# Layer 0's first chunk in split form, and the GpSimd queue written anew around it

## What is computed

```python
B, F, D = (512, 32, 32)
z = jnp.einsum('bhd,bmd->bhmd', x0, prev)   # x0: the gathered rows
z = z.reshape(b, h * m, d)
cur = jnp.einsum('bpd,pn->bnd', z, W[0])    # 128 maps
cur = jax.nn.relu(cur)
...
h = jnp.concatenate([z, dense_ctx], axis=1) # z: both layers summed over d
h = jnp.maximum(h @ W_top1 + b_top1, 0.0)
h = jnp.maximum(h @ W_top2 + b_top2, 0.0)
y = h @ W_top3
```

## Time and profile before

| | |
|---|---|
| median of 3 runs | 843.92 us |
| the profiled execution | 844.84 us |
| its span, first to last instruction | 843.0 us |
| mean granted TensorE clock | 1.00 (2.4 GHz) |
| TensorE busy (matmuls) | 835.0 us, 99% |
| TensorE weight loads busy | 672.6 us, 80% |
| VectorE busy | 770.2 us, 91% |
| ScalarE busy | 784.3 us, 93% |
| GpSimd busy | 723.5 us, 86% |
| DMA traffic | 60.19 MB, mean 71 GB/s |

### The profile page before, as it was taken

How to read it: one execution, slowest core, us unless ns; L and a number is a source line. 1 busy time by engine, 2 the same in 40 slices (tenths; PEclk the granted TensorE clock), 3 DMA queues, 4 the chain that set the end, 5 groups by cost and what they waited for, 6 DMA issues and landing times.

```text
span 843.0 us, 18638 instructions
## 1 busy us (share of the span) xinstructions
PE 835.0 (99%) x3595; PEld 672.6 (80%) x3595; DVE 770.2 (91%) x2029; ACT 784.3 (93%) x2779; POOL 723.5 (86%) x550
## 2 busy tenths in 40 slices
PE   9999999999999999999999999999999999999998
PEld 7688888888888888888888888888888888888777
DVE  7689999999999999999999999999999999999895
ACT  4799999999999999999999999999999999998985
POOL 5898888998888989888999888899888899987860
PEclk9999999999999999999999999999999999999999
DMA  5541233321233332133232123332123333212000
GB/s 150 185 118 38 74 79 85 83 84 42 53 83 80 82 84 57 36 84 78 82 84 71 31 75 78 83 84 82 38 58 82 80 83 84 51 44 77 0 14 1
DMA packets 62104, 60.19 MB, mean 71 GB/s; under 512 B 26203, under 2 KB 37083, under 8 KB 62078
## 3 DMA queue, kind: packets, MB, share of 16 engines
q1 hardware_dynamic: 57982, 57.80, 23.2%
q0 software_dynamic: 4096, 2.11, 4.0%
HBM read 55.51 MB, written 4.31 MB: 71 GB/s over the span
## 4 chain that ended last, share of the span: by engine, by line
PE 93%; POOL 2%; DMA 2%; issue 1%; DVE 1%; SPq 0%; ACT 0%; POOLq 0%; DVEq 0%
PE ps_y L898 26%; PE ps_y L906 26%; PE ps_y L899 26%; PE ps_c L871 3%; PE ps_c L881 3%; PE ps_c L879 2%; PE ps_c L880 2%; POOL gat L453 1%; PE ps_c L877 1%; DMA h_scratch<-h_sums 1%; POOL z L432 1%; DVE prod L728 0%; DMA w_raw<-w 0%; DMA gat<-table,rows 0%; DMA h<-h_scratch 0%
## 5 line engine op out<-in xcount | busy, mean ns | idle before, releaser
L565 ACT ACTIVATE prod<-ps_y,es 128x128 f32<-128x128 f32 x2560 | 723.9, 506 | 34.3 <-PE ps_y L906 27.1
L728 DVE SCALAR_TENSOR_TENSOR prod<-ps_y,es,prod 128x128 f32<-128x128 f32 x1536 | 424.6, 345 | 56.9 <-PE ps_y L906 53.3
L898 PE MATMUL ps_y<-w_hi,c_both 128*128 128x512 f32 x1024 | 415.1, 405 | 1.7 <-POOL w_lo L460 1.3
L906 PE MATMUL ps_y<-w_hi,c_both 128*128 128x512 f32 x1024 | 399.5, 390 | 0.0
L899 PE MATMUL ps_y<-w_lo,c_both 128*128 128x512 f32 x1024 | 399.2, 390 | 0.0
L442 POOL TENSOR_TENSOR prod<-prod 128x768 f32<-128x768 f32 x128 | 238.1, 1860 | 67.2 <-DVE prod L728 64.6
L740 DVE TENSOR_REDUCE csum<-prod 128x64 f32<-128x896 f32 x256 | 276.5, 1080 | 0.1
L898 PEld LDWEIGHTS ps_y<-w_hi,c_both 128*128 128x128 f32 x1024 | 192.4, 188 | 50.9 <-issue 10.3
L899 PEld LDWEIGHTS ps_y<-w_lo,c_both 128*128 128x128 f32 x1024 | 192.4, 188 | 49.4 <-issue 8.2
L906 PEld LDWEIGHTS ps_y<-w_hi,c_both 128*128 128x128 f32 x1024 | 192.2, 188 | 41.6
L432 POOL TENSOR_TENSOR z<-first,second 128x512 f32<-128x512 f32 x155 | 199.0, 1303 | 0.0
(11 more groups left out here) (119 smaller groups left out, 292.7 us busy)
## 6 DMA issues: line engine op xcount, KB each, us to landing
second<-et_scratch SPq DMA_DIRECT2D x155, 256.0 KB, 3.7
first<-et_scratch SPq DMA_DIRECT2D x31, 256.0 KB, 3.4
et_scratch<-gat SPq DMA_DIRECT2D x62, 64.0 KB
w_raw<-w SPq DMA_DIRECT2D x4, 512.0 KB
h_scratch<-h_sums SPq DMA_DIRECT2D x120, 2.0 KB
gat<-table,rows_now POOLq DMA_INDIRECT x116
wt_sb<-wt SPq DMA_DIRECT2D x2, 512.0 KB
rows_now<-rows SPq DMA_DIRECT2D x30, 2.0 KB, 1.8
```

Of the source, the lines that this page charges most:

```text
L565: last = nc.scalar.activation(prod[:, buffer_of(g, u), place // 2, :, place % 2], ps_y[:, bank_of(g, u, k), j * N:(j + 1) * N], ACT.Copy, ...
L728: last = nc.vector.scalar_tensor_tensor(out=summed, in0=ps_y[:, bank_of(g, u, k), j * N:(j + 1) * N], scalar=es[:, g.r, u, h:h + 1], in1=s ...
L898: nc.tensor.matmul(out, hi, w_hi, start=True, stop=False)
L906: nc.tensor.matmul(out, lo, w_hi, start=False, stop=True).then_inc(y_ready, 1)
```

## The change

Chunk 0 of layer 0 takes the split form as well (WHOLE = 0, so SPLIT = 5), which adds a `z_hi` on ScalarE and a `z_lo` on GpSimd per group. Tiles 1 to 3 of all groups but the last are folded by 4 fields in place of 6 (512 elements on GpSimd, and 1024 in place of 896 in each half of VectorE's `reduce`). On GpSimd the fold of a tile stands at the head of the next tile's block, chunk 0 and chunk 1 of group g + 2 are both made in the third tile, and the four gathers stand together in the fourth. `sum_h0` goes from (0, 4) to (1, 4), and the places of layer 0 on TensorE and of `z_hi` on ScalarE are new.

```diff
--- before.py
+++ after.py
@@ -49,7 +49,7 @@
 SLOTS = 3
 BUFS = 3
 LASTK = KP - 1
-WHOLE = 1
+WHOLE = 0
 SPLIT = KP - WHOLE
 UNSPLIT = 2
 WARM_UP = 32
@@ -62,7 +62,7 @@
 PARTNER = {2: 0, 4: 1, 7: 5}
 DVE_BANKS = (tuple(PARTNER),) * TG
 SCALED = HB * len(ACT_BANKS[0])
-FOLD = 6
+FOLD = (6, 4, 4, 4)
 FOLD_LAST = (6, 6, 6, 6)
 HALVES = 2
 
@@ -289,7 +289,7 @@
 
         def fields_folded(g, u):
 
-            return FOLD_LAST[u] if isinstance(g.i, int) and g.times(1) == GROUPS - 1 else FOLD
+            return (FOLD_LAST if isinstance(g.i, int) and g.times(1) == GROUPS - 1 else FOLD)[u]
 
         def place_of(u, k):
 
@@ -402,14 +402,13 @@
 
         @block.gpsimd
         def _(pool):
-            def gather(g, tiles):
-
-                if 0 in tiles:
-                    pool.wait_ge(es_ready, g.times(1, 1 - SLOTS))
-                    wait(pool, et_written, g.times(32, -32 * SLOTS))
-                    pool.wait_ge(rows_staged, g.times(16, 16 * (1 - SLOTS)))
-                    pool.sem_inc(pool_passed, 1)
-                for u in tiles:
+            def gather(g):
+
+                pool.wait_ge(es_ready, g.times(1, 1 - SLOTS))
+                wait(pool, et_written, g.times(32, -32 * SLOTS))
+                pool.wait_ge(rows_staged, g.times(16, 16 * (1 - SLOTS)))
+                pool.sem_inc(pool_passed, 1)
+                for u in range(TG):
                     pool.indirect_dma_start(
                         out=gat[:, g.r, u * D:(u + 1) * D], out_offset=None, in_=table,
                         in_offset=bass.IndirectOffsetOnAxis(ap=rows_now[:, g.r, u:u + 1], axis=0),
@@ -460,24 +459,30 @@
                 nc.gpsimd.tensor_tensor(w1_lo[:, part, :], w1_raw[:, part, :], w1_hi[:, part, :].bitcast(F32),
                                         ALU.subtract).then_inc(w1_last_lo, 1)
 
-            Z_AT_FIRST = {0: ((1, 0), (1, 1), (1, 2)), 1: ((1, 3), (1, 4)), 3: ((2, 0),)}
+            Z_AT_FIRST = {0: ((1, 0), (1, 1), (1, 2)), 1: ((1, 3), (1, 4)), 3: ((2, 0), (2, 1))}
             Z_LO_AT_FIRST = {2: (4,)}
-            Z_AT = {0: ((1, 1), (1, 2), (1, 3)), 1: ((1, 4),), 3: ((2, 0),)}
-            Z_LO_AT = {1: (1, 2), 2: (3, 4)}
+            Z_AT = {0: ((1, 2), (1, 3)), 1: ((1, 4),), 2: ((2, 0), (2, 1))}
+            Z_LO_AT = {0: (0,), 1: (1, 2), 2: (3, 4)}
 
             def body(g, number):
                 more = number is None or number + 1 < GROUPS
-                gathered_at = {2: range(TG)} if number == 0 else {2: (0,), 3: (1, 2, 3)}
+                folds_late = number is None or number < GROUPS - 1
                 for u in range(TG):
+                    if u > 0 and folds_late:
+                        fold(g, u - 1)
+                    if u == 0 and number != 0:
+                        fold(g.plus(-1), TG - 1)
                     products = (Z_AT_FIRST if number == 0 else Z_AT).get(u, ())
                     splits = (Z_LO_AT_FIRST if number == 0 else Z_LO_AT).get(u, ()) if more else ()
                     for n in range(max(len(products), len(splits))):
+                        if u == 2 and n < len(splits):
+                            split_z(g.plus(1), splits[n])
                         if n < len(products) and (number is None or number + products[n][0] < GROUPS):
                             multiply(g.plus(products[n][0]), products[n][1])
-                        if n < len(splits):
+                        if u != 2 and n < len(splits):
                             split_z(g.plus(1), splits[n])
-                    if u in gathered_at and (number is None or number + SLOTS < GROUPS):
-                        gather(g.plus(SLOTS), gathered_at[u])
+                    if u == (2 if number == 0 else 3) and (number is None or number + SLOTS < GROUPS):
+                        gather(g.plus(SLOTS))
                     if (number, u) == (GROUPS - 1, 0):
                         pool.wait_ge(top_hi_ready, 4)
                         pool.wait_ge(folded, LAST.times(TG))
@@ -497,7 +502,8 @@
                         pool.wait_ge(early_h1_hi, 1)
                         nc.gpsimd.tensor_tensor(h1_lo[:, early], h1[:, early], h1_hi[:, early].bitcast(F32),
                                                 ALU.subtract).then_inc(h1_lo_ready, 1)
-                    fold(g, u)
+                    if not folds_late:
+                        fold(g, u)
                     if (number, u) == (GROUPS - 3, 2):
                         pool.wait_ge(top_in, TOP_LOADS * 16)
                         nc.gpsimd.tensor_copy(wt1_hi[:, :, :], wt1_sb[:, :, :]).then_inc(top_hi_ready, 1)
@@ -619,7 +625,7 @@
 
 
             Z_HI_AT_FIRST = {(1, 4): (2, 1)}
-            Z_HI_AT = {(1, 1): (0, 3), (1, 2): (0, 5), (1, 3): (1, 0), (1, 4): (1, 5)}
+            Z_HI_AT = {(1, 0): (0, 0), (1, 1): (0, 3), (1, 2): (0, 6), (1, 3): (1, 1), (1, 4): (1, 5)}
             A1_HI_AT = ((2, 1), (2, 5), (3, 1), (3, 5))
 
             def rectify_a1(j):
@@ -820,7 +826,7 @@
                             reduce(*before(g, u), 0)
                         if number == GROUPS - 1 and (u, k) == (2, 7):
                             reduce(g, 1, 1)
-                        if number != 0 and (u, k) == (0, 4):
+                        if number != 0 and (u, k) == ((0, 4) if number == GROUPS - 1 else (1, 4)):
                             sum_h0(g)
                         if number is None or 0 < number < GROUPS - 1:
                             if (u, k) == (2, 7):
@@ -946,7 +952,7 @@
             other_tiles(0)
 
             Z_USED_AT_FIRST = ((1, 6), (2, 1), (2, 4), (2, 6), (3, 0))
-            Z_USED_AT = ((0, 6), (1, 6), (2, 1), (2, 4), (2, 6))
+            Z_USED_AT = ((1, 1), (2, 0), (2, 2), (2, 5), (2, 7))
 
             def body(g, number):
                 more = number is None or number + 1 < GROUPS
```

## The result

The changed kernel takes **850.79 us**, the median of 4 runs (849.71 to 851.06), against 843.87 for the kernel before in the same comparison: a ratio of 1.0077, 95% interval 1.0065 to 1.0089. It is slower by 6.9 us (850.79 - 843.87), where 6.4 less were forecast. The profiled execution has a span of 849.0 us at a granted clock of 1.00 (2.4 GHz), so the clock plays no part.

A forecast was written before the change was run, and what follows sets the result against it. TensorE, 93% of the chain, was taken to set the pace. Matmuls -5.1, end -2.0, bank stall +0.6 and last group +0.14 sum to -6.4 us: 837.5 us from 843.92, range 835.9 to 841.2.

The forecast's parts named there:

- The step that failed: ScalarE: one added z_hi of 0.52 us makes 24.62 us of work in a 24.87 period, 0.25 left.
- The tight place: VectorE's bank (3, 7) to TensorE's load for (0, 5): 0.13 us left, late by 0 to 0.15; +0.6 us in all.
- leaves 0.6: VectorE's idle 1.59 us a group, less 0.79 for longer reductions and 0.17 for the shorter period, leaves 0.6.
- The matmuls: TensorE's layer 0, chunk 0: split form saves 0.17 us in each of 30 groups, 5.1 us (bounds 4.8 and 6.0).
- The end: Near 780 us, TensorE's stall for late products and z_lo goes: -2.0 us (bounds -2.0 and 0).
- GpSimd at nothing: GpSimd's new order, added z_lo, shorter folds and the fetch of `second` cost 0 us, bounds 0 and 0.
- rival 4: ScalarE and VectorE take the pace, possibly through GpSimd's added z_lo interfering with VectorE: slower, 848.0 us; chance 0.07.
- (2): The stall near 780 us stays in part, as z_lo of chunk 0 joins GpSimd's block 0: 839.5 us; chance 0.10.
- (3): TensorE's layer 0 matmuls do not get shorter, only the end's 2 us are gained: 841.9 us; chance 0.05.
- rival 1: A small stall at bank (0, 5) in every group, 0.08 to 0.15 us each: 839.3 to 841.4 us; chance 0.18.

The follow-up runs named there:

- unroll: The changed kernel with its loop written out on all engines, so without a jump back; 842.46 us, ratio 0.9971.
- lean: The changed kernel without three of ScalarE's five waits for l0_done, 9 instructions fewer in the loop; 839.94 us, ratio 0.9954.
- afold6: The changed kernel with all folds of 6 fields, so VectorE's reductions are short again; 846.66 us, ratio 1.0029.
- unrollfold6: `unroll` with all folds of 6 fields, ScalarE's waits kept; 837.11 us, ratio 0.9911.
- a117: The changed kernel with 117 more ScalarE instructions (met waits) ahead of its untouched loop; 857.05 us, ratio 1.0152.
- a130: `a117` with 13 more ScalarE instructions ahead of the loop; 859.24 us, ratio 1.0181.
- leanfold6: `lean` with all folds of 6 fields, so VectorE's reductions stay at 896 elements; 836.92 us, ratio 0.9908.
- whole: The changed kernel with chunk 0 whole again, folds and order kept except GpSimd's two early products in the fourth tile; 842.76 us, ratio 0.9981.
- afar: The changed kernel with 65 more ScalarE instructions (130 met waits) ahead of its loop; 862.7 us, ratio 1.0207.
- lean120: `lean` with 120 more ScalarE instructions ahead of its loop; 843.85 us, ratio 0.9990.

## Why the prediction was wrong

**The step that failed** is "ScalarE gets one `z_hi` more, which holds it for ... 0.52 us" and "It fits". It priced the engine's work alone, and the work did fit. An instruction added inside a loop is code too: three per group, and two ahead of the loop, carried its end from 580 to 591, past a place where code is fetched ahead. Against `unroll` the stops cost 850.79 - 842.46 = 8.3 us, against the shift in `lean` 12.4, and with short reductions (`afold6` to `unrollfold6`) 9.5; only between `a117` and `a130`, which something else holds back, are they 2.2. With the reductions' 5.35, of which 0.6 was forecast, the first makes 13.05 of the 13.3 between forecast and measurement. Taken in the other order, the reductions are 4.1 and the stops 9.5; the sum is the same. The Trainium skill's sentence on branches, cited above, was there to be weighed, and a row of the page that could have raised the question, q14 with 17 packets and none in the steady part, was not asked.

**The tight place** was found where it is, (3, 7) to the load of (0, 5), and named as the weakest margin; its term was mis-sized. I took 0.02 a group, 0.6 in all, bounds 0 to 4.5. Measured: 0.09 a group in `lean` against `leanfold6` (3.0 us), 4.1 in `afold6`, 5.35 in `unroll`. Each of six reductions is 0.13 longer, as forecast. VectorE's sum of idle time, "leaves 0.6", came true as well: in `lean` it is 2.8% of 24.93, 0.7 us. It didn't keep the weight load at (0, 5) from waiting, so it said nothing about that place.

**The matmuls**: 0.21 a group, not 0.17, so 6.3 us and not 5.1, just outside the bounds 4.8 to 6.0. By the four passes of the Trainium skill (FP8 and Floating Point Precision, TensorE Precision Notes) it would have been 0.23, an estimate nearer than my reading of one start-to-start distance; for 30 groups that is 6.9 us, where the prediction has 6.8. **The end**: 27.09 to 24.91, of which 0.21 is the split, so 2.0, as forecast. **GpSimd at nothing** held: the DMA of `second` kept it waiting 1.6 us in the whole run, its landing went from 3.7 to 4.4 us, and groups of 24.84 stand beside a GpSimd that is 95.4% busy. Its `z_lo` takes 1305 ns against 1300, so the shared port named under rival 4 shows nothing here. The Trainium skill's sentence on it (Advanced Engine Details and Errata, VectorE Performance Modes) is on VectorE instructions in the two-port modes alone, a condition that the prediction left out, and no run here shows in which mode VectorE works.

**Rivals.** (2) fell with the 24.91 us near 780, and (3) with the 0.21 between `whole` and `leanfold6`. The range's upper end, 841.2, was to be that of rival 1, whose own sum gives 841.4; nothing hangs on it. (1) is what the change does without stops: `lean` 839.94 and `unroll` 842.46 in and 1.1 above its 839.3 to 841.4. (4) had the sign, the place (ScalarE's first tile, then VectorE, then the bank) and nearly the time, 848.0, for a reason that isn't so: `lean` does the same work, with ScalarE 98.3% and VectorE 97.2% busy, and its groups average 24.93. It got 0.07; a chance for it as a mere path of lateness, whatever starts it, should have been larger, since ScalarE at 24.62 of 24.87 recovers from a delay at 0.25 a group only.

One remainder: the terms as measured, -6.3 and -2.0, make 8.3 us. `leanfold6` (836.92) is 7.9 below the kernel before in its own comparison (844.85), and `unrollfold6` (837.11) 7.6 below (844.74). Of the 0.4 to 0.7 that are missing, 0.5 stand between groups 1 and 2, at 24.16 us instead of 23.69.

## What to carry to other kernels

In a loop an instruction has two prices, its time on the engine and what it does to the loop's place in the code. Before adding any, look at the packets of the code-fetching queues and at the time between an engine's jump and its next instruction; a profile may name a releaser there that is not the cause. Waits that other waits imply are worth leaving out of a full loop, since each is an instruction there; and where two engines stand above 95%, a longer instruction costs by the room at its place, not by the idle sum.

## What the hardware showed that I had not expected

- The same 367 instructions run without a stop at 215 to 582 and with 3.0 to 3.4 us of stop at 219 to 586: 4 instructions' difference is worth 13 us (844.58 against 857.53). Adding 117 more took stops away again.
- A loop that stops fetches 5 packets of 8192 bytes a turn, two or three of them at the jump and the rest 128 instructions apart: five times 128 for a body of 376. The Trainium skill (Runtime: NRT & Kernel Launch, Instruction fetch mechanics) has blocks of 16 KiB; the packets that recur here are of 8, and the measurement decides for ScalarE. Packets of 16384 bytes are q8's alone, 9 in the looped kernels and 32 in the unrolled ones. Why two places can be passed and three can't, no run shows; only that it sorts all the looped kernels run here. In other words, a loop runs through where its start lies up to 252 instructions behind the last such place (`a117`, 584 - 332) and stops where that is 304 or more (`afar`, 584 - 280); no run lies between.
- TensorE's loop of some 830 instructions never stopped: 0.27 to 0.30 us lie behind its jumps.
- ScalarE's waits that are long met are not free where ScalarE leads the start-up: 130 of them (`afar`) put the first jump 9 us later. But 241 (`lean120`) put it only 3.4 later than in `lean`. The difference is in the pauses between them, whose cause no run shows.
